# Taking the maximum of the second quantisation one iteration later: the vector queue of a pipelined feed-forward stage

## What is computed

```
x = x + layernorm(linear_attention(layernorm(x)) @ W_o)
h = layernorm(layernorm(x), gamma, beta)          # two layernorms in a row
h = qlinear(h, w1, b1)                            # 1024 -> 4096
h = gelu(h)
h = qlinear(h, w2, b2)                            # 4096 -> 1024
x = x + layernorm(h)

def qlinear(x, w, b):      # the scale needs the maximum of a whole row
    sx = 127 / max(|x|, axis=-1);  xq = clip(round(x * sx), -128, 127)
    sw = 1 / mean(|w|);            wq = clip(round(w * sw), -1, 1)
    return xq @ wq.T / (sx * sw) + b
```

## Time and profile before

| | us |
|---|---|
| median of 2 runs | 3546.68 (3545.76 to 3547.6) |
| the profiled execution, whole | 3539.16 |
| its span, slowest core (core 5) | 3537.6 |
| spans of the eight cores | 3511.7 to 3537.6 |

### The profile page before, as it was taken

One profiled execution on the slowest core, in us unless ns is written; L12 is line 12 of the kernel. 1 busy time (PEld: TensorE's weight loads), 2 busy tenths in 40 slices (PEclk: granted clock), 3 DMA queues, 4 the chain that ended last, 5 costly groups with the idle time before them and its releaser, 6 DMA issues.

```text
span 3537.6 us, 33891 instructions; the slowest of 8 cores (3511.7 to 3537.6 us)
## 1 busy us (share of the span) xinstructions
PE 2125.0 (60%) x10640; PEld 1044.8 (30%) x10640; DVE 1538.6 (43%) x2492; ACT 725.3 (21%) x1193; POOL 145.7 (4%) x203
## 2 busy tenths in 40 slices
PE   0161576746667367647667377637867366647676
PEld 0041444412222144413222144412322234312222
DVE  0575534345544143445453134454543243355542
ACT  0030312112221112212222122212221122122221
POOL 0141300000000000000000000000000000000000
PEclk9999576667888666768888667668888676678887
DMA  9897901121111311131111311131111311031111
GB/s 190 248 196 237 189 20 32 28 101 30 42 40 30 134 28 28 26 106 30 36 42 35 129 28 24 28 113 36 27 36 39 128 26 35 21 107 36 42 31 42
DMA packets 333137, 245.50 MB, mean 69 GB/s; under 512 B 304272, under 2 KB 304288, under 8 KB 328864
## 3 DMA queue, kind: packets, MB, share of 16 engines
q0 software_dynamic: 97440, 184.58, 18.8%
q1 hardware_dynamic: 235520, 58.74, 8.7%
HBM read 159.41 MB, written 33.55 MB: 55 GB/s over the span
## 4 chain that ended last, share of the span: by engine, by line
PE 45%; DMA 23%; DVE 16%; ACT 7%; issue 7%; DVEq 1%; another core or an unknown queue 0%; SPq 0%; ACTq 0%; POOLq 0%; POOL 0%; PEldq 0%; PEld 0%
PE pb L906 15%; PE pb L988 14%; DMA abf<-abf 8%; PE pb L492 6%; DMA af<-x 5%; DMA af<-w 4%; PE pb L499 3%; DMA w2q_t<-w2qs 3%; PE pb L909 2%; DMA out<-x 2%; DMA w2qs<-abf 1%; DMA wqkv_t<-w_qkv 1%; DVE abf L576 1%; DVE af L569 1%; DVE khs L532 1%
## 5 line engine op out<-in xcount | busy, mean ns | idle before, releaser
L906 PE MATMUL pb<-w1q_t,abf 128*128 128x512 fp8e4 x2048 | 548.8, 416 | 435.4 <-DMA abf<-abf 435.4
L988 PE MATMUL pb<-w2q_t,abf 128*128 128x512 fp8e4 x2048 | 503.2, 409 | 64.9 <-ACT s2rowr L977 64.9
L906 PEld LDWEIGHTS pb<-w1q_t,abf 128*128 128x128 bf16 x2048 | 192.0, 104 | 717.0 <-issue 564.4
L492 PE MATMUL pb<-abf,wqkv_t 128*128 128x128 bf16 x2048 | 197.5, 289 | 254.9 <-DMA abf<-abf 254.9
L921 DVE TENSOR_REDUCE khs<-af 128x1 f32<-128x1024 f32 x128 | 156.2, 1220 | 409.4 <-ACT af L917 310.9
L988 PEld LDWEIGHTS pb<-w2q_t,abf 128*128 128x128 bf16 x2048 | 208.0, 104 | 342.0 <-issue 144.2
L492 PEld LDWEIGHTS pb<-abf,wqkv_t 128*128 128x128 bf16 x2048 | 192.9, 136 | 259.0 <-issue 259.0
L528 DVE TENSOR_REDUCE khs<-pb 128x8 f32<-128x512 f32 x32 | 22.1, 692 | 440.0 <-ACT af L509 440.0
L917 ACT ACTIVATE af<-pb,scal 128x512 f32<-128x512 f32 x256 | 162.1, 684 | 250.7 <-PE pb L909 250.3
L294 DVE TENSOR_REDUCE af<-af 128x1 f32<-128x4096 f32 x16 | 70.7, 4420 | 146.7 <-DMA af<-w 146.7
L1001 ACT ACTIVATE af<-pb,scal 128x512 f32<-128x512 f32 x32 | 22.0, 687 | 533.5 <-PE pb L992 533.5
(11 more groups left out here) (162 smaller groups left out, 2738.9 us busy)
## 6 DMA issues: line engine op xcount, KB each, us to landing
af<-w POOLq DMA_DIRECT2D x16, 2048.0 KB, 10.0
wqkv_t<-qkvs POOLq DMA_DIRECT2D x3, 6144.0 KB, 21.5
af<-w POOLq DMA_DIRECT2D x32, 512.0 KB, 5.2
af<-w POOLq DMA_DIRECT2D x16, 1024.0 KB, 10.1
af<-x POOLq DMA_DIRECT2D x32, 512.0 KB, 3.9
w1q_t<-w1qs POOLq DMA_DIRECT2D x4, 4096.0 KB, 14.7
w2q_t<-w2qs POOLq DMA_DIRECT2D x4, 4096.0 KB, 23.9
out<-x POOLq DMA_DIRECT2D x32, 512.0 KB, 2.9
```

The costliest lines, as they stand in the source:

```text
L492: mi = PE.matmul(pq, lhsT=wqkv[:, kk, m * 128:(m + 1) * 128], rhs=hf[:, kk, :], start=(kk == 0), stop=(kk == 7))
L906: PE.matmul(Bk[bb0 + n2][:, :], lhsT=xf[:, kk, :], rhs=w1q[:, kk, hs0:hs0 + 512], start=(kk == 0), stop=False)
L988: mi = PE.matmul(Bk[4 + n2][:, :], lhsT=xq2_fm[:, kk, :], rhs=w2q[:, kk, n2 * 512:n2 * 512 + 512], start=(kk == 0), stop=False)
```

## The change

Only the feed-forward stage of each segment is touched. The four waits and maxima over the GELU's output (`qp0` to `qp3`) leave the end of each slab in `f_f1(gg)` and become the first thing in `f_q2(gg)`. The call of `f_q2` moves: group 0 was quantised ahead of the loop and group gg+1 after `f_f2(gg)`; now group gg is quantised in iteration gg, after `f_front_tp(gg+1)` and ahead of `f_front(gg+2)`. No instruction is added or dropped, and all have the sizes they had.

```diff
@@ f_f1 / f_q2
                 ac_mark(ai); ms[f"ac_gel_{seg}_{gg}_{slab}"] = cnt["ac"]
+
+        def f_q2(gg):
+            r = gg % 4
+            for slab in range(4):
                 V.wait_ge(s_ac, ms[f"ac_gel_{seg}_{gg}_{slab}"])
                 vo(f"qp{slab}", [], lambda slab=slab: V.tensor_reduce(
                     out=khs[:, r, 60 + slab:61 + slab],
                     in_=g_sb[:, slab * 1024:(slab + 1) * 1024],
                     axis=AX.X, op=ALU.max, apply_absolute_value=True))
-
-        def f_q2(gg):
-            r = gg % 4
             vo("qm2", ["qp0", "qp1", "qp2", "qp3"], lambda: V.tensor_reduce(
@@ the loop
         f_f1(0)
-        f_q2(0)
         for gg in range(G):
             if gg + 1 < G:
                 f_front_tp(gg + 1)
+            f_q2(gg)
             if gg + 2 < G:
                 f_front(gg + 2)
             if gg + 1 < G:
                 f_f1(gg + 1)
             f_f2(gg)
-            if gg + 1 < G:
-                f_q2(gg + 1)
             if gg >= 1:
                 f_tail(gg - 1)
         f_tail(G - 1)
```

## The result

| | before | after |
|---|---|---|
| median, us | 3546.81 (8 runs, 3540.37 to 3554.6) | 3642.73 (9 runs, 3632.38 to 3650.86) |
| ratio to before | | 1.0266 (95% interval 1.0248 to 1.0284) |
| span of the profiled core | 3537.6 | 3642.3 |
| DVE busy, us | 1538.6 | 1538.6 |
| PE busy, us | 2125.0 | 2122.8 |

A forecast was written before the change was run, and what follows sets the result against it. Bound: the first matmul's transposing DMA, held by a finished group's store. Stops +131, stage ends +66 and starts -60 sum to +137 us on the 3546.7 median: 3684 us, +3.9%, range 3620 to 3730.

The forecast's parts named there:

- The tail stands ahead of q2 and waits for f2: VectorE's queue: second quantisation waits behind a tail until the second matmul's result is out; DVE idles about 25 us there.
- The store still holds the transpose in the middle intervals: Between second and first matmul: the xq1 transpose waits for group k-2's store, so the first matmul starts at 13.6 us.
- The rival that freed the transpose: Before the first matmul: xq1's transpose no longer waits for the store, starting 12.0 us earlier in 20 intervals; 3313 us, chance 0.04.
- A stop of 5.3 us ahead of slab 2: Inside the first matmul, intervals 2 to 5 of each stage: PE waits 5.3 us for the GELU to free slab 0's bank.
- 2.9 us of clock for each stop: After each PE stop in intervals 2 to 5: half clock costs 2.9 us more, making 8.2 per stop, +131 us over 16.
- The lower bound of the term: Stop and clock in intervals 2 to 5: at least 5.2 us each, with clock cost 1.7 and the second matmul's own 1.7 gone.
- The rival without a clock cost: Stops ahead of slab 2 cost only their own 5.3 us, 85 in place of 131; 3638 us, chance 0.10.
- The end, +16.6 a stage: Interval 7, between a stage's last two second matmuls: the last quantisation stands behind tail(5); +16.6 us each, +66 in all.
- The start, -15 a stage: Intervals 0 and 1: the first matmul starts sooner as its transpose goes first; gains 7 and 8 us, -60 in all.
- Interval 6, nothing: Interval 6 of each stage: no front follows the quantisation, so ACT is free for the GELU; change 0.
- No stop: Ahead of slab 2: with DVE's chain 5.3 us shorter, the GELU is there in time; +6 us, 3553 us, chance 0.06.
- the clock stays down: After each of 16 stops: half clock to the end of the second matmul, +17.8 us each; 3969 us, chance 0.04.

The follow-up runs named there:

- the tail inside f2: Changed kernel with the tail of gg-1 written inside the second matmul of gg, ahead of the passes that empty its PSUM banks: 3205.8 us, ratio 0.9029.
- the tail of gg-2 moved: Changed kernel with the tail of gg-2 between quantisation of gg and front of gg+2, replacing the tail of gg-1 at the iteration's end: 3295.2 us, ratio 0.9287.
- The short maxima: Changed kernel with each of the four maxima taken over 64 of its 1024 columns, output no longer the reference's: ratio 0.9941.
- the three above: Changed kernel with maxima over 64 columns, with the last maximum taken twice, or with it taken five times: ratios 0.9941, 1.0328 and 1.0607.

## Why the prediction was right in its mechanism, and where its size was off

- *The tail stands ahead of q2 and waits for f2.* Right. DVE's wait in the tail, foretold at some 25 us, is 24.05 in the interval shown, and writing ScalarE's part of the tail ahead of its wait for f2 takes the ratio from 1.0266 to 0.9029 (the tail inside f2).
- *The store still holds the transpose in the middle intervals.* Right: 13.4 us of idle time ahead of f1 in 20 intervals. The rival that freed the transpose was wrong for this text, and right for another: with the tail written behind the transpose it came to 3295 us (the tail of gg-2 moved), close to the 3313 it had been priced at, but that closeness is luck: it has a stop of 5.2 us that the rival had left out, and it doesn't pay the 66 us at the end of the stages that the rival had counted.
- *A stop of 5.3 us ahead of slab 2.* Right: the 20 waits of 130.0 us hold four of interval 0, 11.36 to 11.72; the other sixteen have 84.2 us, 5.26 each.
- *2.9 us of clock for each stop.* This is the term that was mis-sized. The middle intervals grew by 5.9, not 8.2 (so their period is 57, not the foretold 59 to 60): 5.3 of stop and 0.7 of clock in the net. After the stop, slabs 2 and 3 took 10.5 us in the mean, where two slabs at the full clock take 8.65: 1.9 us, of which the first group of eight has 1.5 (3.42 in place of 1.90). And 1.3 us came back at f2, which had lost 1.7 us to the clock in all 16 middle intervals before and did so in 4 of 16 after. One interval later than the one shown above:

```profile
976.84 10.52 PE L989 MATMUL pb<-w2q_t,abf 128*128 128x512 fp8e4 x48 [1.60 <-ACT s2rowr L978]
```

  Over 16 stops the difference is some 37 us, nearly all of the 41 by which the forecast was too high (137 against 96). The price had been read from an f2, the one after 5.14 us of idle time with 13.45 us, and not from f1, whose start after 13.4 us of idle time costs 2.2 us by the prediction's own rows (two slabs in 10.8 us instead of 8.6). And f2's own 1.7 was left as it was, except in the lower bound. For the same 5.14 us of idle time the trace of before had another value in its third stage, beside 13.40 to 13.45 in the other three:

```profile
1942.65 13.45 PE L988 MATMUL pb<-w2q_t,abf 128*128 128x512 fp8e4 x48 [5.14 <-ACT s2rowr L977]
...
2724.17 11.82 PE L988 MATMUL pb<-w2q_t,abf 128*128 128x512 fp8e4 x48 [5.14 <-ACT s2rowr L977]
```

  so that the same idle time costs 1.3 or 2.9 us. The mean of the four, 2.5, would have taken only 6 of the 37 us away. The lower bound of the term (5.2 for stop and clock) had allowed for a cost of 1.7 with f2's own gone, which is near what came.
- *The rival without a clock cost* gave 3638 us, next to the measured 3642.7, yet that closeness is luck, since its mechanism is not what happened: no stop of the changed kernel was free of clock cost (1.9 us each), and two thirds of that cost came back at f2. The short maxima show what a stop without one looks like (1.89 us for the group).
- *The rule of the Trainium skill* ("TensorE: Matmul & The Clock Gate", section "What's actually happening") puts the ramp at less than 1% of a typical kernel span and advises against fitting a count of slow matmuls. With a stop priced at its own length the term would have been 85 us, where it measured 95 (16 x 5.9). As a forecast that did better than the row chosen. As a statement the rows of this kernel don't bear it out: at every f1 of a middle interval, in both kernels, the first eight matmuls take 3.48 to 3.57 us instead of 1.90. In the kernel before, 20 starts of f1 at 2.2 us and 24 f2 at 1.7 make some 85 us, 2.4% of the span.
- *The end, +16.6 a stage.* Right: +16.3, and f2(7) 21.9 us after f2(6) in the first stage. *The start, -15 a stage.* -16.2, near the upper end given: f1(2) and f2(0) started at the full clock. *Interval 6, nothing.* Right, +0.2.
- *No stop; the clock stays down.* Neither happened. In the changed kernel and in the four experiments with other stop lengths (the three above and the tail inside f2) the third group of eight after each stop took 1.90 us again.

## What to carry to other kernels

When a block of work moves in an in-order queue, look at what it now stands behind, and at what that instruction in turn stands behind on the other engine; here two instructions of ScalarE written ahead of a wait instead of behind it took the time from 2.7% above the kernel before to 9.7% below it. A wait that a helper puts on "all that stands before it in the text" (here the exclusion of stores and transposes) makes the place of a call a dependency: the same reordering loses 2.7% or gains 7% depending on whether the tail is written ahead of the transpose and the quantisation or behind both. And before a price is multiplied by sixteen, it should be taken from the operation that will pay it, and set against what the operations behind it get back.

## What the runs showed of the hardware that was not expected

TensorE's clock did not fall as soon as the matmuls ceased, and how much a stop costs depends on where it falls. In the changed kernel the last matmul before the stop ended at 902.2, and the granted clock was still 1.00 up to 906.0, 3.8 us later (busy times in short stretches; the third column from the right is the granted clock):

```profile
905.00:906.00 1.00, 0.00 (x0) 0.00 (x0) 0.93 (x2) 0.99 (x2) 0.00 (x0) 1.00 0.03 8
906.00:907.00 1.00, 0.00 (x0) 0.00 (x0) 0.93 (x2) 1.00 (x3) 0.00 (x0) 0.73 0.00 0
907.00:908.00 1.00, 0.84 (x3) 0.32 (x4) 1.00 (x1) 1.00 (x3) 0.00 (x0) 0.50 0.00 0
...
909.00:910.00 1.00, 1.00 (x5) 0.29 (x2) 0.84 (x3) 0.00 (x0) 0.00 (x0) 0.56 0.00 0
910.00:911.00 1.00, 1.00 (x5) 0.30 (x4) 0.70 (x5) 0.00 (x0) 0.00 (x0) 1.00 0.00 0
```

It was at half, 1.2 GHz, for some 3.4 us here, and for some 6.8 around the start of the f2 of the earlier trace rows. Idle times of 1.60 us ahead of f2 cost 1.7 us in all 16 middle intervals before and in 4 of the 16 after; stops of 0.4 to 1.7 us ahead of slab 2 cost nothing. With the tail of gg-2 moved, stops of one length (5.15 or 5.16 us) were followed by a first group of 3.32 us in one interval and of 3.57 us in another. Which of two equal idle times pays was not tried by itself and stays open.
